# Conditioned linear attention on one core: bias rows by full-width products, a shorter inverse square root, reordered DVE work, and silu's low parts moved from POOL to DVE

## What is computed

```python
xn = _ln(x, ln_w, ln_b)                       # x: (2, 2048, 512)
q = xn @ Wq + bq
k = xn @ Wk + bk + (1.0 - src_mask) * -1000000.0
q = softmax(q.reshape(b, t, h, dh), axis=-1)  # 8 heads of 64
k = softmax(k.reshape(b, t, h, dh), axis=1)
v = ((xn @ Wv + bv) * src_mask).reshape(b, t, h, dh)
att = einsum('bnhd,bnhl->bhdl', k, v)
y = einsum('bnhd,bhdl->bnhl', q, att).reshape(b, t, d)
emb_out = (silu(emb) @ W_emb + b_emb)[:, None, :]
scale, shift = split(emb_out, 2, axis=2)
hh = _ln(y, ln2_w, ln2_b) * (1.0 + scale) + shift
hh = silu(hh) @ W_out + b_out
return x + hh
```

## Time and profile before

| | us |
|---|---|
| median of 3 runs | 471.68 (471.06 to 471.79) |
| the profiled execution | 471.03 |
| its span in the trace | 469.2 |
| PE busy | 456.6 (97%) |
| DVE busy | 350.0 (75%) |
| ACT busy | 256.6 (55%) |
| POOL busy | 137.5 (29%) |

### The profile page before, as it was taken

How to read it: one execution, slowest core, us unless ns; L and a number is a source line. 1 busy time by engine, 2 the same in 40 slices (tenths; PEclk the granted TensorE clock), 3 DMA queues, 4 the chain that set the end, 5 groups by cost and what they waited for, 6 DMA issues and landing times.

```text
span 469.2 us, 7307 instructions
## 1 busy us (share of the span) xinstructions
PE 456.6 (97%) x2490; PEld 370.8 (79%) x2490; DVE 350.0 (75%) x860; ACT 256.6 (55%) x473; POOL 137.5 (29%) x152
## 2 busy tenths in 40 slices
PE   4999999999999999999999999999999999999997
PEld 2677876886788778888888888888868868888886
DVE  6879866776977956979678667577998727887852
ACT  5634333322787423347555556656789913776671
POOL 0413311120200000104333333334311132785775
PEclk9999999999999999999999999999999999999999
DMA  7966310113232200110213221321322031333222
GB/s 253 352 233 214 118 45 16 40 41 107 65 116 90 91 26 21 47 45 1 68 45 113 70 87 29 110 90 46 135 71 87 0 118 73 105 129 124 97 100 89
DMA packets 23187, 43.49 MB, mean 93 GB/s; under 512 B 1960, under 2 KB 2288, under 8 KB 23152
## 3 DMA queue, kind: packets, MB, share of 16 engines
q1 hardware_dynamic: 22592, 41.98, 26.3%
q10 hardware_dynamic: 560, 1.05, 0.7%
HBM read 34.64 MB, written 8.39 MB: 92 GB/s over the span
## 4 chain that ended last, share of the span: by engine, by line
PE 90%; DVE 6%; issue 2%; DMA 1%; ACT 1%; ACTq 0%; DVEq 0%
PE ps L1219 23%; PE ps L1221 23%; PE ps L1220 23%; PE ps L1224 9%; PE ps L1404 6%; PE ps L1326 2%; DVE ek_lo L861 1%; DMA y<-in_L_cond_Wk_dram 1%; PE ps L1279 1%; PE ps L1382 1%; DVE kf L856 1%; PE ps L1298 1%; DVE zm_lo L851 1%; DVE qs L820 1%; PE ps L1287 0%
## 5 line engine op out<-in xcount | busy, mean ns | idle before, releaser
L629 POOL TENSOR_TENSOR qs<-qs,qmax 128x512 f32<-128x512 f32 x32 | 35.6, 1112 | 170.9 <-DVE qmax L825 170.9
L1219 PE MATMUL ps<-wk_hi,zT_hi 128*128 128x512 f32 x124 | 51.2, 413 | 1.3 <-DVE kf L806 1.3
L1219 PE MATMUL ps<-ek_hi,zm_hi 128*128 128x512 f32 x128 | 50.7, 396 | 1.6 <-DVE ek_lo L861 1.3
L1219 PE MATMUL ps<-wq_hi,zT_hi 128*128 128x512 f32 x128 | 51.8, 405 | 0.0
L1221 PE MATMUL ps<-wq_hi,zT_lo 128*128 128x512 f32 x128 | 50.1, 392 | 0.0
L1220 PE MATMUL ps<-wq_lo,zT_hi 128*128 128x512 f32 x128 | 49.9, 390 | 0.0
L1221 PE MATMUL ps<-ek_hi,zm_lo 128*128 128x512 f32 x128 | 49.9, 390 | 0.0
L1220 PE MATMUL ps<-ek_lo,zm_hi 128*128 128x512 f32 x128 | 49.9, 390 | 0.0
L338 ACT ACTIVATE zT_hi<-ps 128x512 fp32r<-128x512 f32 x32 | 19.1, 597 | 54.7 <-PE ps L1224 54.7
L1221 PE MATMUL ps<-wk_hi,zT_lo 128*128 128x512 f32 x124 | 48.7, 393 | 0.0
L1220 PE MATMUL ps<-wk_lo,zT_hi 128*128 128x512 f32 x124 | 48.4, 390 | 0.0
(11 more groups left out here) (241 smaller groups left out, 1153.1 us busy)
## 6 DMA issues: line engine op xcount, KB each, us to landing
x_in<-in_x_dram SPq DMA_DIRECT2D x35, 512.0 KB, 3.5
res<-in_x_dram SPq DMA_DIRECT2D x24, 256.0 KB, 2.8
out_dram<-res SPq DMA_DIRECT2D x24, 256.0 KB, 2.0
out_dram<-x_in SPq DMA_DIRECT2D x7, 256.0 KB, 2.0
y<-in_L_cond_Wk_dram ACTq DMA_DIRECT2D x2, 512.0 KB, 5.4
kf<-in_L_cond_Wq_dram SPq DMA_DIRECT2D x1, 1024.0 KB, 5.1
eq<-in_L_cond_W_out_dram SPq DMA_DIRECT2D x1, 1024.0 KB, 10.0
wv_mod<-in_L_cond_Wv_dram SPq DMA_DIRECT2D x1, 1024.0 KB, 12.2
```

The lines of the kernel that those rows point to most:

```text
L629: pool.tensor_tensor(q_heads, q_heads, qmax[:, n % 2, :].unsqueeze(2).broadcast_to([P, H, DH]), ALU.subtract).then_inc(s["q_shift"], 1)
L1219: pe.matmul(o, a[0], bb[0], start=start, stop=False)
```

## The change

Five edits are made together.

1. The bias rows of q and v are made as that of k is: `bias_sum` now issues four products with a 128x128 left operand, summed in one bank. `bias_parts`, ACT's two copies and the sum by 1/32 go.
2. `finish_part` on DVE uses a rule of higher order for the first two rounds together, then one round of Newton's: 9 instructions instead of 10, of which two don't wait for each other. POOL's own root (`y_root`) stays.
3. In the first batch's keys and queries, `k_tile(0, 4)` comes before the statistics of two x tiles.
4. Around the start of the first batch's state, DVE does `masked_z(0, 2)` and `k_less_max(0, 2)` earlier, and the two last `q_top`, with POOL's `q_shift` and ACT's `exp_q` behind them, later.
5. `h_low` of tiles 12, 13 and 14 (in stretch 4) and of 20 to 31 (the second batch's fifth tile on, in stretch 5) is done by DVE instead of POOL; one `silu` and one `h_high` of stretch 4 move by one step.

```diff
-                if n == 1:
-                    exp_q(0, T - 1)
+                if n in (1, 2):
+                    exp_q(0, T - 3 + n)
...
-                if n == 5:
+                if n == 6:
                     h_high(HT + 1)
...
-            for m in range(HT, T - 1):
-                h_low(m)
...
             for m in range(T, 2 * T):
-                h_low(m)
+                if m < T + 4:
+                    h_low(m)
...
+                v, a, root = st["v"][:, of], st["a"][:, of], st["y"][:, of].bitcast(F32)
+                if k == 1:
+                    link(dve.tensor_tensor(st["b"][:, of], v, root, ALU.mult))
+                    here()
+                    link(dve.tensor_tensor(a, st["b"][:, of], root, ALU.mult))
+                    link(dve.tensor_tensor(r, st["b"][:, of], root, ALU.mult))
+                    return
+                if k == 2:
+                    link(dve.scalar_tensor_tensor(out=st["b"][:, of], in0=r, scalar=-10 / 3, in1=a, op0=ALU.add, op1=ALU.mult))
+                    here()
+                    link(dve.scalar_tensor_tensor(out=r, in0=st["b"][:, of], scalar=5.0, in1=root, op0=ALU.add, op1=ALU.mult))
+                    return
...
+            def h_low(m):
+                dve.wait_ge(s["h_hi_ok"], m + 1)
+                dve.wait_ge(s["h_lo_ok"], m)
+                if m >= T:
+                    dve.wait_ge(s["o_ps"], m - 3)
+                dve.tensor_tensor(h_lo(m), th_of(m), h_hi(m).bitcast(F32), ALU.subtract).then_inc(s["h_lo_ok"], 1)
...
+                if n == 4:
+                    k_tile(0, n)
                 if n > 3:
                     x_part(0, n)
...
             masked_z(0, 1)
             keys_top(0)
+            masked_z(0, 2)
             k_less_max(0, 0)
             k_less_max(0, 1)
             zm_low(0, 0)
             q_add(0, T - 2)
             ek_low(0, 0)
-            q_top(0, T - 2)
             zm_low(0, 1)
+            k_less_max(0, 2)
             ek_low(0, 1)
             q_add(0, T - 1)
-            masked_z(0, 2)
-            k_less_max(0, 2)
-            q_top(0, T - 1)
...
             def next_tokens(n):
+                if n < 2:
+                    q_top(0, T - 2 + n)
...
                 if n == 5:
+                    h_low(HT)
+                if n == 6:
                     silu(HT + 1)
+                if n == 8:
+                    h_low(HT + 1)
                 if n == 10:
                     silu(HT + 2)
+                if n == 12:
+                    h_low(HT + 2)
...
+                if T + 3 < m + 2 < 2 * T:
+                    h_low(m + 2)
...
-            def bias_parts(by, raw, done):
+            def bias_sum(bank, by, raw, done):
 
                 for f in range(NB):
-                    last = pe.matmul(ps[32 * f:32 * f + 32, YTB, :], by[:, f:f + 1].broadcast_to([P, 32]), raw[:, f, :],
-                                     start=True, stop=True)
+                    last = pe.matmul(ps[:, bank, :], by[:, f:f + 1].broadcast_to([P, P]), raw[:, f, :],
+                                     start=(f == 0), stop=(f == NB - 1))
                 last.then_inc(s[done], 1)
...
-            bias_parts(cols[:, LNB:LNB + NB], wq_raw, "bq_part")
             product_q(0, 0)
-            pe.wait_ge(s["bq_copy"], 1)
-            pe.wait_ge(s["part_ok"], 1)
-            pe.wait_ge(s["cols_ok"], 2)
-            bias_sum("bq_ps")
+            bias_sum(YTB, cols[:, LNB:LNB + NB], wq_raw, "bq_ps")
...
-                    bias_parts(lnb_w, wv_mod, "bv_part")
-                if n == 8:
-                    pe.wait_ge(s["bv_copy"], 1)
-                    bias_sum("bv_ps")
+                    pe.wait_ge(s["cols_ok"], 2)
+                    bias_sum(YB + 1, lnb_w, wv_mod, "bv_ps")
```

More of the change, by code:

```diff
@@ L195, in cond_linear_attention @@
         wq_scaled = eq[:, 0:4]
-        bias_part, bv_all = kf[:, 15, :], kf[:, 14, :]
+        bv_all = kf[:, 14, :]
         wemb = [eq[:, 10 + t, :] for t in range(4)] + [kf[:, 10 + t, :] for t in range(4)] + \
@@ L204, in cond_linear_attention @@
         names = """table_ok ln_in vec_in wk_in0 wk_in1 wq_in wv_in wo_in bk_in bq_in bias_in ident0 ident_ok part_ok ones_ok pick_ok
-            vec_ps cols_ok lnbw_ok kb_ps bq_part bq_copy bq_ps bv_part bv_copy bv_ps bk_ok bq_ok row_ok
+            vec_ps cols_ok lnbw_ok kb_ps bq_ps bv_ps bk_ok bq_ok row_ok
             wk_hi_ok wk_lo_ok wq_hi_ok wq_scaled wq_lo_ok wv_ok wo_hi_ok wo_lo_ok
@@ L494, in _ @@
                 copy(wq_scaled[:, f, :], wq_raw[:, f, :], "wq_scaled", ln_weight(f))
-            act.wait_ge(s["bq_part"], 1)
-            copy(bias_part, ps[:, YTB, :], "bq_copy")
             normalise_x(0, 2)
@@ L516, in _ @@
                     copy(emb_rows[0], ps[:, YTB, :], "emb_ok")
-                if n == 8:
-                    act.wait_ge(s["bv_part"], 1)
-                    copy(bias_part, ps[:, YTB, :], "bv_copy")
             for n in range(2):
@@ L525, in _ @@
                 ek_high(0, n)
-            exp_q(0, T - 2)
             act.wait_ge(s["emb_ps"], 2)
@@ L739, in finish_part @@
                     return
-                root = st["y"][:, of].bitcast(F32) if k == 1 else r
-                link(dve.tensor_tensor(st["b"][:, of], st["v"][:, of], root, ALU.mult))
+                v, a, root = st["v"][:, of], st["a"][:, of], st["y"][:, of].bitcast(F32)
[10 more added lines that the diff above has]
+                    return
+                link(dve.tensor_tensor(st["b"][:, of], v, r, ALU.mult))
                 here()
-                link(dve.scalar_tensor_tensor(out=st["a"][:, of], in0=st["b"][:, of], scalar=-0.5, in1=root, op0=ALU.mult, op1=ALU.mult))
+                link(dve.scalar_tensor_tensor(out=a, in0=st["b"][:, of], scalar=-0.5 * 0.375 ** 3, in1=r, op0=ALU.mult, op1=ALU.mult))
                 here()
[L745 to L749, removed]
+                link(dve.scalar_tensor_tensor(out=r, in0=a, scalar=1.5 * 0.375, in1=r, op0=ALU.add, op1=ALU.mult))
+                here()
+                dve.scalar_tensor_tensor(out=shift, in0=st["mv"][:, of, 0], scalar=-1.0, in1=r,
+                                         op0=ALU.mult, op1=ALU.mult).then_inc(s[done], 1)
             def xst_of(b, c):
@@ L1030, in _ @@
             dve.wait_ge(s["bq_ps"], 1)
-            dve.tensor_tensor(bq_all[:], bq_all[:], ps[:, YB + 1, :], ALU.add).then_inc(s["bq_ok"], 1)
+            dve.tensor_tensor(bq_all[:], bq_all[:], ps[:, YTB, :], ALU.add).then_inc(s["bq_ok"], 1)
             dve.wait_ge(s["bq_ok"], 1)
@@ L1057, in _ @@
                     dve.wait_ge(s["wv_ok"], NB)
-                k_tile(0, n)
+                if n != 4:
+                    k_tile(0, n)
                 if n < T - 2:
@@ L1282, in key_bias @@
                     last.then_inc(s["kb_ps"], 1)
-            def bias_parts(by, raw, done):
+            def bias_sum(bank, by, raw, done):
                 for f in range(NB):
-                    last = pe.matmul(ps[32 * f:32 * f + 32, YTB, :], by[:, f:f + 1].broadcast_to([P, 32]), raw[:, f, :],
-                                     start=True, stop=True)
+                    last = pe.matmul(ps[:, bank, :], by[:, f:f + 1].broadcast_to([P, P]), raw[:, f, :],
+                                     start=(f == 0), stop=(f == NB - 1))
                 last.then_inc(s[done], 1)
-            def bias_sum(done):
-                pe.matmul(ps[:, YB + 1, :], part[:], bias_part, start=True, stop=True).then_inc(s[done], 1)
             def condition(h):
```

## The result

The changed kernel is slower. Its median is 474.31 us (473.17 to 475.04, 6 runs) beside 471.58 (471.06 to 471.94, 6 runs) of the kernel before on the same chips, a ratio of 1.0051 with a 95% interval of 1.0038 to 1.0065. By the ratio that is 2.4 us more, between 1.8 and 3.1 (the two medians differ by 2.7). The forecast was 472.9, so the direction was right and the size half of what came. The median lies 0.2 above the upper end of the range, 474.1; the ratio, set on the 471.68 that the forecast started from, gives 474.1, the end itself. The profiled execution took 473.55 us with a span of 471.8.

A forecast was written before the change was run, and what follows sets the result against it. PE, busy 456.6 of 469.2 us, was taken to bound the kernel. +3.07 - 0.43 - 0.37 - 1.10 + 0.1 = +1.27 (edit 2 at nothing), on the median 471.68, gave 472.9; range 471.4 to 474.1.

The forecast's parts named there:

- the rival of the other side: Bias rows of q and v: PE's longer rows are absorbed, 3.07 off the sum, 469.9 us; chance 0.09.
- POOL starts its next subtraction 0.1 to 0.2 behind it, and `ek_lo(3)` meets it exactly as before: First batch's state, fourth tile: `ek_lo(3)` is held up, a new PE wait of 0.55 + 0.11; edit 4 nets -0.37.
- the gaps close fully: Both states: `ek_lo(3)` misses POOL or PE comes late; edit 4 brings 1.03, edit 5 up to 1.38; 471.9 us; chance 0.20.
- behind it the bias add itself comes 1.6 later, since its load waits for that store, and the meeting doesn't recur: Last stretch, from tile 20: only one DVE low part is blocked by POOL's bias add, costing 0.1; bounds 0 and +1.5.
- The second rival: Last stretch: blocked low parts on DVE delay `out_tile`, PE waits at several tiles; +2.7, 474.4 us; chance 0.12.
- PE waits for `out_tile` in the last stretch: Sign of being wrong, last stretch: PE waits for `h_lo` or for `out_tile` there; no size given.
- the fourth tile has no wait: Sign of being wrong, first batch's state: the forecast wait of about 0.5 for `ek_lo` at the fourth tile is missing.

The follow-up runs named there:

- b_bias: The kernel before with edit 1 alone, four full-width products for each bias row of q and v: ratio 1.0063 against the kernel before.
- a_old_root: The changed kernel with the old inverse root on DVE, edit 2 undone: ratio 1.0055 against the kernel before.
- b_last: The kernel before with only the low parts of tiles 20 to 31 moved to DVE: ratio 1.0051 against the kernel before.
- a_tiny: The changed kernel with POOL adding the last eight tiles' output bias in one column of 512 only: ratio 1.0000 against the kernel before.
- b_ktile: The kernel before with edit 3 alone, k_tile(0, 4) ahead of the statistics of two x tiles: ratio 0.9999 against the kernel before.
- a_best_k: a_best with k's bias row made by narrow products as well: 468.75 us, ratio 0.9929 against the kernel before.
- a_paced: The changed kernel with POOL's bias add, from m = 20 on, waiting for DVE's low part of tile m: ratio 1.0004 against the kernel before.
- a_again: The changed kernel once more, unchanged: ratio 1.0058 against the kernel before.
- a_best: The changed kernel without edit 1 and with the last stretch's low parts on POOL: 468.20 us, ratio 0.9928 against the kernel before.

## Why the prediction was half right

1. **Edit 1** was read rightly: +3.07 forecast, 2.84 by the trace and 2.97 by the timing of b_bias alone. The term came from distances of starts in the same kernel, and no wait absorbed it, so the rival of the other side is out. Some 0.1 of the rest is seen at q's row: behind k's row the product with Wq and what follows it came 1.18 earlier (5.45 us from 17.11 to 22.56, against 6.63 from 17.10 to 23.73), not 1.09.
2. **Edit 2**: forecast 0, bounds 0 to -0.3; undone in the changed kernel (a_old_root) it is worth 0.3 us, the lower bound; by what the other edits leave of the third stretch it is worth 0.15. Either way it works in that stretch, not in edit 3's neighbourhood.
3. **Edit 3**: -0.43 forecast, -0.37 by the trace.
4. **Edit 4**: -0.37 forecast, -1.23 measured. The step that failed is "POOL starts its next subtraction 0.1 to 0.2 behind it, and `ek_lo(3)` meets it exactly as before". The offsets were as forecast, to 0.1 us; which of the two instructions gives way was not. The rival "the gaps close fully" is what happened here.
5. **Edit 5 in the state**: -1.10 forecast, -1.02 measured.
6. **Edit 5 in the last stretch**: +0.1 forecast with a bound of +1.5, +2.5 to +2.6 measured. At tile 20 the forecast was right in kind and size: where the meeting happened the low part took 1.66 (b_last, a_tiny) or 1.55 (a_old_root), the low parts behind it 0.68, and the stretch was at most 0.1 longer. The step that failed is "behind it the bias add itself comes 1.6 later, since its load waits for that store, and the meeting doesn't recur". It was worked out at tile 20, where the rows of x pass through the three `res` buffers and so pace POOL, and carried on to tile 31. From tile 24 on the rows lie in `x_in` and nothing paced POOL but the low parts that the edit took from it. That could have been read from the program text and from the kernel before's trace, where POOL does a low part and a bias add in turn. The second rival had the mechanism, blocked low parts that delay `out_tile`, with a chance of 0.12 and 1.1 us too cheap. That its 474.4 is the measured 474.3 is luck: what it left out, edit 4's further 0.9, edit 2's 0.15 and the 0.2 too much for edit 1, came to as much.

Summed from the trace: 2.84 - 0.37 - 1.23 - 1.02 - 0.15 + 2.6 = +2.7, beside 471.8 - 469.2 = 2.6 of the spans (0.15 for the root is what is left of the state's 2.40). Two errors of opposite sign, -0.9 in the state and +2.5 in the last stretch, left the forecast 1.3 us low; without the first it would have been 2.2 low. Of the signs of being wrong that it named, two stand in the profile: PE waits for `out_tile` in the last stretch, and the fourth tile has no wait.

The Trainium skill's page "SBUF — State Buffer", section Who interferes with whom, has the rule behind points 4 and 6: the second to issue fully blocks. By it the low part of tile 26 has to wait for the bias add that runs, and 1.78 for 0.68 agrees. The low part of tile 25 agrees too: the add that ran had 0.23 us left, and it lost only 0.10. At 128.62, though, the trace has `ek_lo(3)` issue last of the three and not wait at all, while POOL's subtraction, issued before it, takes 2.02. So for low parts that stand back to back the rule tells that one of the two will pay, and here the trace had to tell which.

## What to carry to other kernels

When work is taken off an engine, ask what had been pacing the rest of its queue. POOL's low parts had spaced its bias adds; without them eight adds ran in one burst, and two of DVE's instructions paid 1.1 us each for it. A wait that holds the lighter engine back can be worth more than the work it delays: here one added wait brought 2.45 us. And check a mechanism at each kind of tile it is carried over to, above all where buffers change.

Where edits come in a bundle, measure them alone. Here four parts gained (2.8 us together) and two lost (5.4); the bundle hid both, and leaving out the two losing ones beats both kernels.

## What the runs showed that I had not expected

- The same three instructions with the same offsets (0.16 and 0.60 us) held up DVE in one order of the program (`ek_lo` 1.53 or 1.54, POOL 1.42) and POOL in the other (`ek_lo` 0.68, POOL 2.02 or 2.03). Both outcomes are stable: the first in all five kernels with the old order, the second in all nine of the new order. What decides it stays open.
- At the very start PE's first full products stand 0.43 apart in some executions and 0.23 in others, with a granted clock of 1.00 in the profile's rows for both. With waits of 0.96 and 0.77 us for ACT's normalised x ahead of them (b_ktile, a_best_k) the wide distance lasted until 12.4 and at least 13.7. But the wait alone doesn't decide it: with one of 0.20 it lasted until 12.7 in a_paced, with one of 0.24 it was gone after the first product in b_bias. Without any it lasted until 11.9 in a_again and 12.2 in the changed kernel, and was gone after the first product, or never there, in the rest. It cost up to 1.3 us: from the first of these products to the first behind them takes 14.93 - 10.11 = 4.82 us in a_best_k and 13.82 - 10.27 = 3.55 in a_best. The ratio of the distances, 1.9, is close to that of the two levels of PE's clock, 1.2 and 2.4 GHz, but the profile's rows have the granted clock at 1.00 throughout. No experiment was made on its cause.
